# Moving one VectorE product between the two state scans of a pair, in a four-layer post-norm kernel

## What is computed

```python
x = _layernorm(x + _L0_attn_ref(x, ...))   # decayed linear attention
x = _layernorm(x + _L0_ffn_ref(x, ...))    # silu(x W1) * (x W3), Hadamard transform, W2
x = _layernorm(x + _L1_attn_ref(x, ...))   # selective scan
x = _layernorm(x + _L1_ffn_ref(x, ...))    # silu(gate) * up, w_down
```

```python
def step(h, inp):
    delta_t, B_t, C_t, u_t = inp
    dA = jnp.exp(delta_t[:, :, None] * A[None])
    dBu = (delta_t * u_t)[:, :, None] * B_t[:, None, :]
    h = dA * h + dBu
    y_t = jnp.einsum('bdn,bn->bd', h, C_t)
    return (h, y_t)
```

## Time and profile before

| | |
|---|---|
| median of three runs | 1828.31 us |
| the profiled execution, own time | 1820.48 us |
| its span, first to last instruction | 1818.7 us |
| scan's stretch | 537 to 1640 us of the span |
| TensorE busy over the span | 1736.3 us (95%) |
| VectorE | 1241.6 us (68%) |
| ScalarE | 1120.5 us (62%) |
| GpSimd | 1194.6 us (66%) |
| mean granted TensorE clock | 0.994 |

### The profile page before, as it was taken

The page is one execution under the profiler, slowest core; times in us unless marked ns, Lnnn a source line. Parts: engine busy times, 40 slices in busy tenths (PEclk is TensorE's granted clock), DMA queues, the critical chain, the costliest instruction groups (busy, mean ns, idle before and its releaser), DMA issues. The chain is left out here.

```text
span 1818.7 us, 26882 instructions
## 1 busy us (share of the span) xinstructions
PE 1736.3 (95%) x9472; PEld 1134.8 (62%) x9472; DVE 1241.6 (68%) x1336; ACT 1120.5 (62%) x1721; POOL 1194.6 (66%) x932
## 2 busy tenths in 40 slices
PE   7999999799989999999999999998999999999998
PEld 5666666577756665565555665554656566667786
DVE  2524443323139999999899999987999999982212
ACT  5453443566577777867767777676776767653212
POOL 4634433355528877899887997788987988772111
PEclk9999999999999999999999999999999999999999
DMA  7443423487858987788776997777877787864652
GB/s 254 135 130 97 148 65 126 170 297 260 298 169 297 320 310 268 256 294 307 249 258 239 318 311 259 241 262 248 279 283 275 261 276 261 290 225 165 206 194 93
DMA packets 160023, 427.07 MB, mean 235 GB/s; under 512 B 31888, under 2 KB 54992, under 8 KB 159504
## 3 DMA queue, kind: packets, MB, share of 16 engines
q1 hardware_dynamic: 159888, 425.34, 68.6%
HBM read 356.07 MB, written 69.21 MB: 234 GB/s over the span
## 5 line engine op out<-in xcount | busy, mean ns | idle before, releaser
L1885 POOL TENSOR_TENSOR q_or_raw_or_h_times_c<-h_states,c_rep 128x512 f32<-128x512 f32 x293 | 375.5, 1296 | 50.0 <-DVE h_states L1775 45.2
L1650 ACT ACTIVATE decay<-delta_on_states,a_neg 128x512 f32<-128x512 f32 x512 | 350.2, 716 | 44.2 <-DMA delta_on_states<-delta 39.9
L1760 DVE TENSOR_TENSOR du_spread_in_d_b<-du_spread_in_d_b,b_rep 128x1024 f32<-128x1024 f32 x256 | 310.3, 1212 | 30.8 <-PE du_spread_in_d_b L1472 28.3
L1775 DVE TENSOR_TENSOR_SCAN h_states<-decay,h_last,du_spread_in_d_b 128x512 f32<-128x512 f32 x256 | 317.7, 1270 | 9.0 <-ACT h_last L1655 2.3
L1885 POOL TENSOR_TENSOR h_times_c_rest<-h_states,c_rep 128x512 f32<-128x512 f32 x219 | 282.2, 1300 | 55.7 <-DVE h_states L1775 47.6
L1775 DVE TENSOR_TENSOR_SCAN h_states<-decay,du_spread_in_d_b 128x512 f32<-128x512 f32 x256 | 302.2, 1209 | 18.4 <-ACT h_last L1655 12.3
L1837 POOL TENSOR_TENSOR h_lo<-v_or_silu_in_h_lo,h_hi 128x512 fp32r<-128x512 f32 x128 | 166.9, 1304 | 204.3 <-ACT h_hi L1552 203.3
L111 PE MATMUL y_or_aux<-h_hi,w 128*128 128x512 f32 x468 | 193.9, 414 | 10.9 <-POOL h_lo L1837 10.7
L1725 DVE TENSOR_TENSOR v_or_silu_in_h_lo<-v_or_silu_in_h_lo,up_or_scores 128x512 f32<-128x512 f32 x128 | 86.9, 679 | 146.0 <-PE up_or_scores L113 131.5
L113 PE MATMUL y_or_aux<-h_hi,w 128*128 128x512 f32 x468 | 183.4, 392 | 0.0
L112 PE MATMUL y_or_aux<-h_lo,w 128*128 128x512 f32 x468 | 182.8, 391 | 0.0
(11 more groups left out here) (240 smaller groups left out, 3840.0 us busy)
## 6 DMA issues: line engine op xcount, KB each, us to landing
delta_on_states<-delta SPq DMA_DIRECT2D x256, 512.0 KB, 5.8
w<-w_split SPq DMA_DIRECT2D x112, 512.0 KB, 5.6
attn_w_hi_or_x_hi_w<-w_split SPq DMA_DIRECT2D x112, 512.0 KB, 5.2
attn_w_lo_or_x_lo_w<-w_split SPq DMA_DIRECT2D x112, 512.0 KB, 5.4
w_split<-w_presplit_hi_lo SPq DMA_DIRECT2D x32, 512.0 KB, 4.0
w_presplit_hi_lo<-in_w13b SPq DMA_DIRECT2D x32, 256.0 KB, 3.5
w_split<-attn_w_hi_or_x_hi_w SPq DMA_DIRECT2D x8, 1024.0 KB, 6.6
w_split<-attn_w_lo_or_x_lo_w SPq DMA_DIRECT2D x8, 1024.0 KB, 6.6
```

The source lines that it names most:

```text
L1650: act.activation(da[:, s % ND], dring[:, s % NR], ACT.Exp, scale=a[:, column(s):column(s) + 1]).then_inc(s_da, 1)
L1760: dve.tensor_tensor(both, both, brep[:, tile_of(s // SPO) % 2].unsqueeze(1).to_broadcast([P, 2, TT]), ALU.mult).then_inc(s_db, 1)
L1775: dve.tensor_tensor_scan(hs[:, s % NH], da[:, s % ND], uu[:, s % NU], initial, ALU.mult, ALU.add).then_inc(s_hs, 1)
L1885: pool.tensor_tensor(hc[s % NC_], hs[:, s % NH], crep[:, tile_of(s // SPO) % 2], ALU.mult).then_inc(s_hc, 1)
```

## The change

`inject(p)` moves from behind scan 2p-1 to between scan 2p-2 and scan 2p-1. `spread_inputs(p)` moves from step 2p-1 to step 2p-2; its wait, on scan 2p-3, stays. LAG goes from 4 to 5, so that `sum_states` and `leave` come one step later. VectorE's queue now reads: scan 2p-2, inject p, scan 2p-1, scan 2p, inject p+1, scan 2p+1. Numbers of instructions, their sizes and the buffers stay.

```diff
-    ND, NU, NH, NC_, NR, LAG = 6, 4, 6, 7, 6, 4
+    ND, NU, NH, NC_, NR, LAG = 6, 4, 6, 7, 6, 5
...
                         s = step_at(tick, half)
-                        if s >= -1 and s % 2 == 1 and s + 1 < STEPS:
-                            spread_inputs((s + 1) // 2)
+                        if s == -1:
+                            spread_inputs(0)
+                        if s >= 0 and s % 2 == 0 and s + 2 < STEPS:
+                            spread_inputs(s // 2 + 1)
                         if s >= LAG and (s - LAG) % JB == JB - 1 and s - LAG < STEPS:
                             sum_states((s - LAG) // JB)
...
                 def step(s):
                     if 0 <= s < STEPS:
                         scan(s)
-                    if 0 <= s + 1 < STEPS and s % 2 == 1:
-                        inject((s + 1) // 2)
+                    if s == -1:
+                        inject(0)
+                    if s >= 0 and s % 2 == 0 and s + 2 < STEPS:
+                        inject(s // 2 + 1)
                     if SPO <= s < STEPS and s % SPO == LAG + 1 or s == STEPS + LAG:
                         leave(s // SPO - 1)
```

## The result

The changed kernel takes 1841.93 us (median of 4, 1838.92 to 1845.19), beside it the kernel before 1828.09 (median of 4, 1826.38 to 1829.96). The ratio is 1.0078 [1.0059, 1.0097]: the change makes it slower by 14 us. The profiled execution took 1843.01 us, its span is 1841.2 us. The two profiled executions are 22.5 us apart, but 5.1 of these lie ahead of the scan, where nothing was changed (the first spread stands at 536.8 us of before and at 541.9 of after); the other 17.4 come later, with the scan.

A forecast was written before the change was run, and what follows sets the result against it. TensorE was taken to set the pace in the scan. VectorE's saving -2.5, LAG 5 -4 and the spread's wait +8.5 gave +2 us on the median 1828.3: 1830.3 us, own range 1824.7 to 1832.0, 8-in-10 range 1815 to 1845.

The forecast's parts named there:

- rival 2: TensorE and VectorE in lock-step at the spread's wait for scan 2p-3: +12 us (17 - 5), 1840 us; chance 0.29.
- VectorE's saving: In VectorE's queue, 147 scans directly behind their inject each start 0.18 us sooner: 26 us of VectorE's time, taken as -2.5 us.
- rival 3: On VectorE, scans still start 1.30 us behind an inject, so nothing is saved: +16 us, 1844 us; chance 0.04.
- LAG 5: State sums one step later on TensorE give GpSimd's product more room: bounds 0 to 7.0 us, taken as -4 us.
- The cost to GpSimd: GpSimd's waits for later sums could delay low parts of h: bounds 0 and 15 us, taken as 0, covered by idle time.
- low parts that grow behind waits for sums: Sign on GpSimd: the prediction is wrong if waits for low parts of h grow because GpSimd waits for sums; costed at nothing.
- Spread and sum together: On TensorE, spread and sum still follow each other, now at even steps, taking 1.63 us as before: nothing.
- The spread's wait: TensorE's spread, one step sooner, waits for scan 2p-3, which ends 0.94 us later: bounds 0 and 23 us, taken as 8.5 us.
- its five large ones: Five largest expected shortfalls at TensorE's spreads, at 617, 810, 557, 1130 and 903 us, together 7.5 us.

The follow-up runs named there:

- e2: Changed kernel with VectorE's order put back as before, so only the early spreads and LAG 5 remain: 1.0025 of the kernel before, 1832.05 us.
- e6: Changed kernel with LAG back at 4, so sums stand at odd steps apart from spreads: 1.012 of the kernel before, 1847.82 us.
- e9: Changed kernel with the inject at half its width, the product for the other tokens left out: 1.0014 of the kernel before, 1828.79 us.
- e8: Kernel before with the inject at half its width, the product for the other tokens left out: 0.9968 of the kernel before, 1820.82 us.
- e3: Kernel before with only the inject moved as in the change, spreads at odd steps and LAG 4 kept: 1.0247 of the kernel before, 1872.04 us.
- e4: Changed kernel with spreads and sums issued half a tick (three matmuls) later on TensorE: 1.018 of the kernel before, 1859.23 us.
- e12: Changed kernel with LAG 3, sums still beside the spreads at even steps: 1.0123 of the kernel before, 1848.35 us.
- e5: Kernel before with LAG 6 instead of 4, nothing else changed: 1.0185 of the kernel before, 1860.48 us.

## Why the prediction was right or wrong, step by step

Forecast was no measurable change (1830.3), measured is +13.8 us. The range of 1815 to 1845 us held it, but that range held a gain and a loss alike. What came is rival 2, the lock-step, which had a chance of 0.29: the waits before L1472 are over 15 us and go on beyond 1260 us (6.3 us in 12 of the 41 there), as it said they would.

**VectorE's saving: right in size.** The pitch from inject to scan is 1389.11 - 1387.99 = 1.12 us, and over 164 adjacent pairs the median is 1.116, where the 147 of the kernel before had 1.297. So rival 3 falls. The Trainium skill, "VectorE: DVE Perf Modes", section "The DRAIN you can't avoid", says of a chain of copies that a semaphore after each costs nothing extra. That is not what this trace shows for inject and scan: an instruction that depends on the one just ahead starts 0.18 us later than one that doesn't. Its worth was taken as 2.5 us. The `add` waits lost 5.8 of the 6.1 us in the view and 7.8 by starts, the silu waits 3.8 by starts; but e2, without the saving, has lost 6.5 and 1.4 of these already. So the saving itself is behind 1.3 us of the `add` waits at most. The likely reason for the rest, that everything ran later behind the waiting spreads, wasn't tested.

**LAG 5: right for the products, the cost left out.** Products -7.1 us where -4 was taken. The cost to GpSimd was put at 0 with idle time as cover; the low parts grew by 2.5 us (5.0 in e2). The step that was wrong in kind is "the sum is long done when it gets there": GpSimd waits 146.6 us for sums, not some 10. The prediction had named low parts that grow behind waits for sums as a sign that it is wrong, and this sign is there. Most of the 146.6 us falls on GpSimd's idle time (it waited 47.6 + 45.2 us for scans before, 5.6 + 3.1 in after), but not all, and TensorE's waits for low parts by LAG are 1.6, 7.8, 13.9 us in the new order (3, 4, 5) and 11.4, 16.4, 31.6 in the old one (4, 5 in e2, 6). The products go the other way, 23.0, 3.6, 0.2 and 7.3, 1.1, 0: what a step of LAG takes from one it gives to the other, but not in equal parts. From 3 to 4 in the new order 19.4 us went and 6.2 came, from e2 to e5 1.1 went and 15.2 came (in e2 the spread is early as well).

**Spread and sum together: right.** Nothing in the changed kernel, and e6 shows the 25 us that it would cost otherwise.

**The spread's wait: the step that failed.** 8.5 us were taken, bounds 0 and 23; measured are 25.6 us in the view and 30.7 by starts. The price was found by moving spreads and scans of the old trace against each other, and was cut from 23 to 8.5 by two sentences: that a wait of TensorE gives the next pairs room "until VectorE has caught up", and that shortfalls of 0.4 us are made good by savings of 0.18. Both take VectorE as an engine that is late by a backlog, which a pause works off. To see whether it was, look at VectorE's unbroken run of work in front of each late spread. For 35 of 53 late spreads of after (20.6 of 30.7 us, by starts) this run began less than 5.5 us before, with a wait of its own: 17 times for a feed-forward matmul, 13 for a spread, 5 for `h_last`. VectorE had caught up fully, and the spread was late all the same, as at 1390 us. By what began the run, in us of late spreads:

| kernel | short run, behind a wait for TensorE | short run, behind `h_last` | longer run |
|---|---|---|---|
| after | 14.0 (30) | 6.6 (5) | 10.2 (18) |
| e2 spreads early only | 1.1 (2) | 3.6 (2) | 9.6 (17) |

The part that a backlog can explain is the same in both. What the moved inject adds stands in short runs, 12.9 us of it behind waits for TensorE. The two largest waits of after, 3.0 us at 1236 and 2.2 at 1199, stand in the middle column: ScalarE made VectorE late there, not TensorE. The larger one, first VectorE, then TensorE:

```profile
1232.14 1.22 DVE L1777 TENSOR_TENSOR_SCAN h_states<-decay,du_spread_in_d_b 128x512 f32<-128x512 f32 x1 [3.05 <-ACT h_last L1657]
```

```profile
1235.66 0.39 PE L1472 MATMUL du_spread_in_d_b<-stack,selectors 24*128 24x512 bf16 x2 [2.97 <-DVE h_states L1777]
```

Nor did the old trace find the places. The spreads of its five large ones (pairs 20, 66, 6, 140 and 86), priced at 7.5 us, wait 0.8 us by starts in after, all five together; the loss is in the many small ones, which had been given 1 us.

VectorE's time saved turned into its own waits (`hidden` 7.8 to 24.0, `add` 12.8 to 24.5 us), since while TensorE stands no input for VectorE is made either.

What is too long in the short runs behind TensorE is the chain from TensorE through VectorE back to TensorE. At 1390 us it starts with a feed-forward sum, done at 1385.77 + 0.39 = 1386.16, and ends with scan 2p-1 at 1390.38: add, scan, inject, scan, 4.2 us. TensorE's own work from the one to the spread lasts to 1390.05, 3.9 us. In the old order the inject would not be in the chain (1.12 us less) and the spread would come a step later (2.15 us more work beside it). e2 takes the step alone (+5 us), the change both (+14), e9 shortens the inject again (+8 over e8), e3 gives the step back but leaves the inject (the wait moves to VectorE), and e4 stands between. That order and early spread, and not the late sums, make most of the wait is shown by e12. The upper bound of 23 was too low by 8 us; it was read at the times of the old trace, in which no instruction of VectorE had yet been held by the new waits. That this is the reason was not tried by itself.

**The sum as measured,** by starts: spreads +30.7, products -7.1, `add` -7.8, silu -3.8, low parts +2.5, issue and other +1.6, together +16. Rival 2 had 17 and -5 for its two sides, where 30.7 and, for products, `add` and silu, 18.7 were measured. Its mechanism came, though by the table above it has 14.0 of the 30.7 us for itself and a backlog or ScalarE had a part in the rest; that its 1840 us lie so near to 1841.9 is luck, two sides taken too small that cancel.

## What to carry to other kernels

When an operation is moved in one in-order queue and its partner in another, write down the closed chain between the two engines and compare its length with the pacing engine's round; slack counted in the old trace and busy shares don't show it. A pause of one engine helps the other to catch up only where that one has a backlog: look at whether its run of work before the late instruction began with a wait of its own. Here 0.18 us saved behind 147 injects didn't pay for the step of distance and the inject in front of the scan. And before a consumer in an in-order queue is put later, look at what else stands in the queue of the engine that has to wait for it: from LAG 4 to 6 the waits moved from the products to the low parts.

## What the runs showed of the hardware

- Small matmuls between full 128x128 ones cost by the number of places, not only by their work: spread and sum at two places take 0.21 us more than at one (e6), 25 us over the scan.
- On VectorE a scan starts 1.30 us behind an inject that it needs (147 places, before) and 1.12 us behind one that it doesn't (164 places, after).
- Behind some of its waits the granted clock of TensorE is at its lower level (1.2 of 2.4 GHz) for a few us. In the kernel before, behind 4.2 us of waiting; columns as in the stretches above:

```profile
1258.60:1260.80 2.20, 2.20 (x7) 1.72 (x6) 1.13 (x2) 2.19 (x5) 2.20 (x3) 0.50 0.87 313
```

  Matmuls of 128x512 start 0.43 us apart there instead of 0.23. Added up from these starts, this costs 2.3 us in before, 4.2 in after, 8.7 in e3, 8.0 in e4 and 7.7 in e5. So some waits cost more than themselves, and the kernels with many show it in the column "issue".
- LAG from 4 to 6, with the same instructions, made the kernel 34 us slower (e5).
